# A gated delta-rule stage: the empty-row test to ScalarE, the inverses ahead of the gated output, the beta sigmoid and two GpSimd steps earlier

## What is computed

```python
mem = DECAY * mem + dt
spike = (mem > THR)                              # forward value; then mem -= spike * THR
alpha = sigmoid(at + asp * spike)                # at = silu(h @ Wau + bau) @ Wad + bad
beta = sigmoid(bt + sum(spike * bsp))
active = sum(abs(spike), -1) > 0                 # per token and head
alpha = where(active, alpha, 1);  beta = beta * active
s = s * alpha;  s = s + (beta * kt) * (vt - kt @ s);  out = qt @ s
```

## Time and profile before

| | |
|---|---|
| runs | 2898.83 us median of 3 (2896.13 to 7392.36) |
| the profiled execution | 2903.73 us, its span 2901.9 us |
| TensorE busy | 2361.8 us (81%), weight loads 1655.3 (57%) |
| VectorE busy | 1634.3 us (56%) |
| ScalarE busy | 969.8 us (33%) |
| GpSimd busy | 732.5 us (25%) |
| granted TensorE clock, mean | 0.829 |
| delta stage, core rounds | about 1150 to 2370 us of the span; the core rounds 1 to 6 take about 155 to 159 us each |

### The profile page before, as it was taken

One profiled execution on the slowest core, in us unless ns is written; L12 is line 12 of the kernel. 1 busy time (PEld: TensorE's weight loads), 2 busy tenths in 40 slices (PEclk: granted clock), 3 DMA queues, 4 the chain that ended last, 5 costly groups with the idle time before them and its releaser, 6 DMA issues. The chain is left out here.

```text
span 2901.9 us, 74066 instructions
## 1 busy us (share of the span) xinstructions
PE 2361.8 (81%) x31128; PEld 1655.3 (57%) x31167; DVE 1634.3 (56%) x4406; ACT 969.8 (33%) x1910; POOL 732.5 (25%) x852
## 2 busy tenths in 40 slices
PE   7898989998778576888989898989988886956674
PEld 4666666666665332555656564656656755745553
DVE  4455555545362474767676676767564713477334
ACT  3343343434212253342424343333434331310222
POOL 0110101101016452424231314232241300112663
PEclk9799898979559786999999998999998975555776
DMA  4000000000021131000000000000000002000114
GB/s 150 9 1 9 9 9 5 1 1 1 7 74 44 47 135 47 3 21 6 21 6 21 6 3 24 3 20 6 2 6 2 7 1 90 2 30 19 44 44 113
DMA packets 42507, 75.80 MB, mean 26 GB/s; under 512 B 5989, under 2 KB 27245, under 8 KB 39621
## 3 DMA queue, kind: packets, MB, share of 16 engines
q1 hardware_dynamic: 35140, 56.63, 5.7%
q0 software_dynamic: 7040, 14.43, 1.8%
HBM read 46.73 MB, written 24.31 MB: 24 GB/s over the span
## 5 line engine op out<-in xcount | busy, mean ns | idle before, releaser
L2630 POOL TENSOR_TENSOR delta_scaled_beta_k<-delta_scaled_beta_k,delta_decays 128x256 f32<-128x256 f32 x160 | 122.1, 763 | 434.0 <-DVE weights_sb L2742 225.2
L2719 DVE COPY_PREDICATED delta_neg_a_and_p_t<-delta_level_int,bank 128x256 f32<-128x256 uint8 x384 | 179.2, 537 | 74.1 <-PE bank L2244 73.2
L2244 PE MATMUL bank<-weights_sb,delta_scaled_beta_k 64*64 64x64 f32 x6144 | 136.1, 234 | 85.6 <-DVE delta_neg_a_and_p_t L2719 79.2
L2268 PEld LDWEIGHTS bank<-delta_inverse,delta_neg_a_and_p_t 64*64 64x64 f32 x5120 | 176.8, 145 | 46.2 <-issue 45.8
L2268 PE MATMUL bank<-delta_inverse,delta_neg_a_and_p_t 64*64 64x64 f32 x5120 | 199.7, 232 | 0.0
L2244 PEld LDWEIGHTS bank<-weights_sb,delta_scaled_beta_k 64*64 64x64 f32 x6144 | 116.0, 145 | 122.6 <-DVE delta_neg_a_and_p_t L2719 98.1
L683 POOL TENSOR_TENSOR attn_probs<-attn_probs,attn_row_sum 128x512 f32<-128x512 f32 x64 | 65.4, 1043 | 397.7 <-DVE attn_row_sum L766 397.7
L2476 ACT ACTIVATE delta_two_less_ax<-bank 128x512 f32<-128x512 f32 x160 | 94.8, 597 | 208.6 <-PE bank L2268 208.4
L303 PE MATMUL bank<-attn_z_self_t,weights_sb 128*128 128x256 f32 x512 | 153.4, 452 | 13.3 <-DVE attn_cross_values L741 9.6
L312 PE MATMUL bank<-attn_w_value_out,attn_z_self_t 128*64 128x512 f32 x512 | 143.0, 684 | 2.1 <-DVE attn_z_value_out L706 1.4
L2150 PE MATMUL bank<-delta_head_rows,norm_sel 16*128 16x512 f32 x192 | 117.6, 712 | 27.2 <-DVE delta_head_rows L2844 19.8
(11 more groups left out here) (535 smaller groups left out, 5325.8 us busy)
## 6 DMA issues: line engine op xcount, KB each, us to landing
delta_drives<-front_drive SPq DMA_DIRECT2D x7, 1024.0 KB, 3.9
weights_sb<-in_w_moe_dram SPq DMA_DIRECT2D x1, 4352.0 KB, 14.7
z_rows<-moe_z_all SPq DMA_DIRECT2D x16, 256.0 KB, 2.3
delta_odd_spikes<-delta_drives SPq DMA_DIRECT2D x4, 1024.0 KB, 5.0
weights_sb<-moe_outs SPq DMA_DIRECT2D x8, 512.0 KB, 7.2
weights_sb<-delta_drives SPq DMA_DIRECT2D x3, 1024.0 KB, 5.1
weights_sb<-in_w_delta_dram SPq DMA_DIRECT2D x1, 2816.0 KB, 9.8
weights_sb<-in_ctx_tok_dram SPq DMA_DIRECT2D x8, 264.0 KB, 5.9
```

What stands on the lines that cost most here:

```text
L2244: last = pe.matmul(two[eo][rows(sg), b4 * 64:b4 * 64 + 64], kr[r, hp, t], second(kq[r, g % 2, :, hp, t], c), start=b < 2, stop=True, skip_ ...
L2268: last = pe.matmul(out_[rows(sg), u], AP[rows(sg), hp, eo, b4, 0, :], X[rows(sg), hp, u], start=False, stop=True, skip_group_check=True)
L2630: pool.tensor_tensor(r_[:, :, 0, :], r_[:, :, 0, :], a_[:, :, 1, 0:1].to_broadcast([128, T // (2 * c), c]), ALU.mult)
L2719: last = dve.copy_predicated(second(AP[:, hp, eo, :, :, :].rearrange("p b i n -> p (b i) n"), c), m_, PAIR[hp % 2][eo][:, :].rearrange("p ...
```

## The change

The empty-row test moves to ScalarE: right behind the copy of the logits it computes relu(1 - count), which is 1 for an empty head and 0 for any other, since counts are whole numbers. The 1e30 moves into the weights `wD[64:72, 4]`. VectorE's f_cb goes, and its f_beta waits for ScalarE's count of `cb_rd`. ScalarE waits for the f_beta of the group before, which reads the rows that it writes. VectorE runs the level-0 masks of all four pairs in a row, then the first inverses, and then the gated output. ScalarE takes f_beta ahead of the last `w_out`. GpSimd does `reset` for the next round and `z_tok` for this group's tokens behind its last scaling, ahead of `spikes`.

```diff
--- before.py
+++ after.py
@@ -2050,6 +2050,7 @@
                 cnt_w = sb("count_and_beta_w", [128, 5, 64], ctx=ctx)
                 bcol = sb("beta_bias", [128, HDP + 1], ctx=ctx)
                 log_eps = sb("log_64_eps", [128, 1], ctx=ctx)
+                ones = sb("one", [128, 1], ctx=ctx)
                 zzT = sb("z_out_t", [128, T], ctx=ctx)
                 hid = sqk
                 tmp = sb("silu_or_square", [128, 2, T], ctx=ctx)
@@ -2506,6 +2507,11 @@
                         if g >= 1:
                             act.wait_ge(s["kr_ps"], nth_of("kr", g - 1, 3))
                         act.activation(hrows[BETA, :], J[at_fill["cb", g, 0] % 2][96:128, :], ACT.Copy).then_inc(s["logit"], 1)
+                        if g >= 1:
+                            act.wait_ge(s["al_ps"], nth_of("al", g - 1, 3))
+                            act.wait_ge(s["beta"], g)
+                        act.activation(au[64:96, :], J[at_fill["cb", g, 0] % 2][64:96, :], ACT.Relu, bias=ones[64:96, :], scale=-1.0)\
+                            .then_inc(s["cb_rd"], 1)
 
                     def t_silu(g, n):
                         act.wait_ge(s["f1_ps"], nth_of("f1", g, n))
@@ -2597,10 +2603,11 @@
                         if ahead:
                             f_au(it + 2)
                         act.preload_act_table(ACT.Sigmoid)
+                        if front:
+                            f_beta(it + 1)
                         if core:
                             w_out(it, 5)
                         if front:
-                            f_beta(it + 1)
                             f_alpha(it + 1)
                         if core:
                             x_out(it, 5)
@@ -2674,10 +2681,6 @@
                     for it in range(-1, NG + 1):
                         core, front, tail = 0 <= it < NG, 0 <= it + 1 < NG, it >= 1
                         if core:
-                            reset(it)
-                        if tail:
-                            z_tok(it - 1)
-                        if core:
                             scale(it, 0)
                         if front:
                             squares("k", it + 1)
@@ -2692,6 +2695,10 @@
                         if core:
                             scale(it, 3)
                             scale(it, 4)
+                        if front:
+                            reset(it + 1)
+                        if core:
+                            z_tok(it)
                             if it + 2 < NG:
                                 spikes(it + 2)
 
@@ -2832,15 +2839,9 @@
                             x_ = kq[:, g % 2, 0, j, :]
                             dve.tensor_tensor(x_, x_, J[at_fill["bk", g, j] % 2][:, :], ALU.mult).then_inc(s["bk_rd"], 1)
 
-                    def f_cb(g):
-                        dve.wait_ge(s["logit"], g + 1)
-                        if g >= 1:
-                            dve.wait_ge(s["al_ps"], nth_of("al", g - 1, 3))
-                        dve.tensor_scalar(au[64:96, :], J[at_fill["cb", g, 0] % 2][64:96, :], 0.0, 1e30, ALU.is_equal, ALU.mult)\
-                            .then_inc(s["cb_rd"], 1)
-
                     def f_beta(g):
                         dve.wait_ge(s["sigmoid"], g + 1)
+                        dve.wait_ge(s["cb_rd"], g + 1)
                         dve.scalar_tensor_tensor(hrows[BETA, :], au[64:96, :], 0.0, hrows[BETA, :], ALU.is_equal, ALU.mult)\
                             .then_inc(s["beta"], 1)
 
@@ -2855,7 +2856,8 @@
                     dve.tensor_tensor(bcol[:, 0:HDP], col("bbeta", 0, HDP), bcol[:, HDP:HDP + 1].to_broadcast([128, HDP]), ALU.mult)
                     for r in (32, 64, 96):
                         dve.tensor_copy(nsel[r:r + 16, 0:HDP, :], nsel[0:16, 0:HDP, :])
-                    dve.tensor_copy(wD[64:72, 4, :], nsel[0:8, 0:HDP, :].rearrange("p j d -> p (j d)"))
+                    dve.tensor_scalar(wD[64:72, 4, :], nsel[0:8, 0:HDP, :].rearrange("p j d -> p (j d)"), 1e30, None, ALU.mult)
+                    dve.memset(ones[:, :], 1.0)
                     dve.wait_ge(s["const_set"], 1)
                     for j in range(HDP):
                         dve.tensor_copy(cnt_w[:, j, 0:16], col("norm_rows", 16 * j, 16))
@@ -2886,20 +2888,14 @@
                             for j in range(HDP):
                                 o_normed(it - 1, j)
                         if core:
-                            for hp in (0, 1):
+                            for hp in range(HDP):
                                 masked(it, 1, hp)
                                 scale(it, 0, hp)
-                        if front:
-                            f_cb(it + 1)
-                        if core:
-                            for hp in (2, 3):
-                                masked(it, 1, hp)
-                                scale(it, 0, hp)
+                            for hp in range(HDP):
+                                first_inverse(it, hp)
                         if tail:
                             t_gated(it - 1)
                         if core:
-                            for hp in range(HDP):
-                                first_inverse(it, hp)
                             for hp in range(HDP):
                                 masked(it, 2, hp)
                                 scale(it, 1, hp)
```

## The result

| | before | after |
|---|---|---|
| median | 2897.48 us | 2805.71 us |
| ratio to before | | 0.9698, 95% interval 0.9658 to 0.9738 |
| the same again, the two side by side on one chip | 2900.35 us | 2807.11 us, 0.967 (0.9627 to 0.9713) |
| profiled span | 2901.9 us | 2801.0 us |
| start of round 0 in the span, first and second profile | 1150.0, 1140.3 | 1127.8, 1138.0 |

The ratio leaves out one of the four runs of before, which took 7392.36 us.

The account below looks back on a forecast made before the run. TensorE was taken as the bound of the delta stage, so its standing and low-clock time could be won. 54 + 8.5 + 1.3 + 11 = 75 us less gave a median of 2824 us; own range 2809 to 2840, overall 2808 to 2851.

Parts of the forecast that it names:

- Part 1: Delta rounds: empty test leaves VectorE, inverses go ahead of gated output; 9.0 us in each of rounds 1 to 6, 54 us.
- the sum: Step-by-step timing of round 3, and the total of all prices: 54 + 8.5 + 1.3 + 11 = 75 us.
- The upper price of 9.2: Rounds 1 to 6, test and inverses moved: W's first matmul 9.2 us earlier; 7.0 if the clock stays low.
- Round 7: No test there; inverses only fill VectorE's 1.39 us wait for the projection: 1.3 us gain.
- Round 0: No output projection there, but the test waited 7.82 us; moving test and inverses gains 8.5 us.
- Part 2: Beta sigmoid ahead of ScalarE's last W copies: 1.5 to 2.2 us a round, taken as 1.6, rounds 0 to 6: 11 us.
- Part 3: GpSimd's reset and z_tok move to the end of the round before: taken at 0, other bound 3.8 us a round.
- Its bound of 3.8 us: VectorE's membrane steps: five GpSimd instructions of 5.0 us in all hold up five steps, costing 3.8 us a round.
- Less clock: Rival: busier TensorE is granted less clock, 0.95 to 0.84 in six full rounds; 2932 us, chance 0.04.
- A wait in place of the other: Rival: second q projection waits if VectorE reaches the gated output later than before (1632.46); 2885 us, chance 0.04.
- The part given back to the membrane steps: Rival: membrane steps held up by GpSimd land on the path, 3.8 us a round; gain 48, 2850 us, chance 0.19.
- Its side case: Held-up membrane steps with low clock after the test and inverse moves beside them: gain said to be about the same 48.

Follow-up runs that it names:

- the best of these kernels: Changed kernel with normalisations between mask pairs, W copies between norm reductions, and 16 instead of 26 membrane steps ahead of level-4 masks: 0.9531 of before, 2764.67 us.
- the kernel with the normalisations between: Changed kernel with the last two of VectorE's four output normalisations behind the level-0 masks of pairs 0 and 1: 0.9651 of before, 2795.88 us.

## Why the prediction was right

**Part 1** was right in mechanism and close in size. VectorE's mask pairs follow each other at once, it waits 1.28 us before the gated output (about 1 forecast; 1.2 in the sum), the masks start behind it, and the 8.5 us that the sum left from the products to W (1630.9 to 1639.4) took 8.14. In round 3 the stretch fell by 9.5 us, over the rounds 1 to 6 by 10.0 on average in the first pair of profiles and 9.8 in the second, against 9.0: 59 to 60 us instead of 54. The upper price of 9.2 came from round 3 alone, and that was one of the shorter stretches of before (21.4 us against 21.9 on average). The dispute between the piece at the low and at the high clock (7.0 or 9.2) was decided for the high one: 1.00 in its row. Round 7 gained 1.4 us, of 1.3. Round 0 was taken too high: for both parts together it had 10.1 us and gained 9.6 and 7.8, of which 2.2 are part 2's, so 5.6 to 7.4 are left of the 8.5. That the two edits belong together was an argument there; the experiments show it, with each alone left at a wait of 4.2 or 5.8 us.

VectorE's slack was as read: of the 3.20 us of idle before its next mask, 1.59 are left (`1.59 <-PE bank L2245` at 1592.93 of the changed kernel's timeline), where the sum had left 2.0.

**Part 2**: TensorE's wait of 2.25 us went, 0.63 us stands before the third W product, and the stretch fell from 18.5 and 18.8 us (means of the rounds 1 to 5 in the two profiles of before, those in which it could be read in both) to 16.9: 1.6 to 1.9 us a round, and 2.2 in round 0, against 1.6. That is 12 to 14 us, of 11; the runs of this edit alone say 15.

**Part 3** was taken at 0 and is 0 within what the runs tell. That part 2 shields it is shown, though by another instruction than the prediction named: without part 2 the reset holds up beta's mask by 0.41 us. Its bound of 3.8 us rested on five GpSimd instructions holding five steps, and one did: the reset held one step for 1.80 us, z_tok none. All membrane instructions together took 190.8 us in the profile of before and 200.6 in that of after, 1.6 us a round more in six rounds. With GpSimd's move alone no step is held so long, as VectorE reaches them when the reset is through (1559.66 against 1559.08), and they took 191.8. By the Trainium skill (SBUF — State Buffer, Who interferes with whom) VectorE with two SBUF inputs and a GpSimd instruction that reads SBUF exclude each other; the trace agrees for the reset (1.80 against 0.22 us, and 1.09 against 0.68) and for GpSimd's squares (0.97), and does not for the four instructions of z_tok, which read SBUF too and beside which steps took 0.21 to 0.27 us.

**The rivals.** Less clock: in the rounds the granted clock was 0.94 and 0.95 in the two profiles of after, against 0.92 and 0.91 before. The 0.84 that the rival took for round 0 is of a stretch that begins 30 us ahead of it; round 0 itself had 0.86, and 0.88 and 0.90 after. The Trainium skill (TensorE: Matmul & The Clock Gate, Part 1: The HAM clock gate) lets the level follow how busy the engine has been; with the 1.00 where the wait of 6.64 us had left 0.53, the trace agrees. A wait in place of the other: not in the changed kernel, where VectorE reaches the gated output with 1.28 us to spare, but in the kernel with the inverses alone, which crosses the stated point. The part given back to the membrane steps: not seen at its 27 us, as the changed kernel without GpSimd's move is no faster by the runs and its rounds are 4 to 6 us shorter. Its side case was added up wrongly: with low clock in part 1 too, the prediction's own terms leave 42 + 8.5 + 1.3 + 11 - 26.6 = 36 us, not 48.

**What was short is the sum**, by 17 us. Part 1's rounds 1 to 6 explain 5 to 6 of them and part 2 up to 3, and round 0 takes 1 to 3 back. The rounds of the two profiles give 78 and 84 us in all, against 73.5. With round 7's 1.4 they leave 8 to 13 of the 92 and 93 us of the runs (8 and 11 of the 88 and 96 of the ratios), in no stretch that repeats: runs of the kernel before on one chip go from 2889.82 to 2912.73 us, and its rounds took 1085.6 and 1092.8 in two profiles. What makes the runs gain more than the rounds stays open.

## What to carry to other kernels

When an engine stands before one instruction while its queue holds work that is ready, look behind that instruction for the work that the bound engine wants, and take the instruction away and let that work pass the next waiting one too: here each edit alone left a wait of 5.8 or 4.2 us and gave 13 and 23 us, both gave 72. Price a wait of the bound engine with the slow work behind it, at the durations of both clock levels, and look at several rounds, since the slow work does not follow each time. After each gain read the waits again: the best of these kernels came from 20 small instructions in front of a mask for which TensorE waited over 3 us only once the W wait of 2.7 us ahead of it was gone.

## What was not expected of the hardware

- One and the same kernel took 2848.95 us on one chip and 2898.24 and 2900.35 us on two others. In the profiles the rounds hardly differ (1086.0 and 1095.7 us with the inverses and with GpSimd's steps alone on the first, 1085.6 and 1092.8 for the kernel before on others). The part behind them does, 631 to 633 us against 663 to 667, and so does the part ahead: round 0 began at 1116.9 to 1127.5 us on the first chip and at 1127.8 to 1150.0 on the others. Why was not tried.
- ScalarE's Relu of 32x512 from PSUM took 0.68 us, as long as VectorE's test (0.69), and longer than its own copy of the same shape (0.59). It brought no table load: each of the three load lines has 11 before and after.
- How short the waits are that can cost a second time, and that they do not always: behind two of 1.27 and 1.03 us four k matmuls took 3.06 us in round 3 and 1.98 in round 5 of the same execution. Behind one of 0.82 us they took 1.98 in round 3 of the kernel with the normalisations between.
